# The down weights of a fused attention and feed-forward kernel: their rotation taken as eight products of rounded halves instead of four full float32 products

## The reference

```python
x = x + _L0_xattn_ref(_layernorm(x), ctx_2048, mask, Wq, bq, Wk, bk, Wv, bv, Wo, bo, gamma, beta, residual_scale)
x = x + _L0_ffn_ref(_layernorm(x), SU_ug, SU_dp, Wscale_ug, Wscale_dp, W_up, W_gate, W_down)

# _L0_ffn_ref
x = fwht(x * SU_ug) / SCALE                     # 512 wide
x_up = x @ W_up.T * (Wscale_ug[:INTER] * SCALE)
x_gate = x @ W_gate.T * (Wscale_ug[INTER:] * SCALE)
x = silu(x_gate) * x_up
x = fwht(x * SU_dp) / SCALE                     # 2048 wide
x = x @ W_down.T * (Wscale_dp * SCALE)
```

## Time and profile before

| | us |
|---|---|
| median of 3 runs | 1454.08 |
| lowest and highest run | 1452.18, 1454.42 |
| the profiled execution | 1452.16 |
| its span, first to last instruction | 1450.3 |
| TensorE busy | 1407.1 (97% of the span) |
| VectorE busy | 1107.4 (76%) |
| ScalarE busy | 814.2 (56%) |

### The profile page before, as it was taken

The page is one execution under the profiler, slowest core; times in us unless marked ns, Lnnn a source line. Parts: engine busy times, 40 slices in busy tenths (PEclk is TensorE's granted clock), DMA queues, the critical chain, the costliest instruction groups (busy, mean ns, idle before and its releaser), DMA issues. The chain is left out here.

```text
span 1450.3 us, 25099 instructions
## 1 busy us (share of the span) xinstructions
PE 1407.1 (97%) x10344; PEld 954.1 (66%) x10344; DVE 1107.4 (76%) x1655; ACT 814.2 (56%) x1018; POOL 88.8 (6%) x128
## 2 busy tenths in 40 slices
PE   7999999999999999999999999998999999999997
PEld 6787333788333688333689333586788888888886
DVE  6953999885999895899885899887866565656654
ACT  5345999535999635899635899534533333333330
POOL 1000000101000100000100000110010010000100
PEclk9999999999999999999999999999999999999999
DMA  8453000536100425000424500362345554454435
GB/s 275 151 185 153 9 10 10 177 104 218 52 10 10 147 98 190 21 17 10 141 74 175 241 17 10 97 240 86 146 147 208 189 182 149 163 208 176 174 145 174
DMA packets 54785, 180.91 MB, mean 125 GB/s; under 512 B 11168, under 2 KB 25760, under 8 KB 42384
## 3 DMA queue, kind: packets, MB, share of 16 engines
q1 hardware_dynamic: 39696, 116.08, 22.2%
q0 software_dynamic: 14976, 63.23, 12.7%
HBM read 111.97 MB, written 67.31 MB: 124 GB/s over the span
## 5 line engine op out<-in xcount | busy, mean ns | idle before, releaser
L960 ACT ACTIVATE cx_probs<-cx_sc,proj_mbias 128x1024 f32<-128x1024 f32 (+1 forms) x416 | 442.7, 1113 | 48.2 <-PE cx_sc L1234 24.6
L1103 DVE TENSOR_SCALAR cx_probs<-cx_probs 128x1024 f32<-128x1024 f32 (+1 forms) x416 | 269.8, 685 | 50.8 <-ACT cx_probs L960 49.0
L1069 DVE TENSOR_TENSOR cx_padd<-cx_probs,cx_probs 128x1024 f32<-128x1024 f32 x192 | 234.0, 1219 | 0.9
L1234 PEld LDWEIGHTS cx_sc<-cx_q,cx_kt 32*128 32x128 f32 (+1 forms) x2496 | 103.7, 180 | 192.2 <-ACT cx_probs L960 172.5
L1257 PE MATMUL cx_acc<-cx_probs,cx_vt 128*32 128x512 f32 (+1 forms) x1664 | 218.1, 596 | 3.8 <-DVE cx_probs L1103 3.8
L1234 PE MATMUL cx_sc<-cx_q,cx_kt 32*128 32x512 f32 (+1 forms) x2496 | 206.5, 425 | 10.2 <-ACT cx_probs L960 7.1
L140 PE MATMUL ff_yp<-hand_wds,ff_held 128*128 128x512 f32 x624 | 143.7, 389 | 0.1
L1702 DVE TENSOR_TENSOR ff_x<-ff_yp,ff_x 128x512 f32<-128x512 f32 x128 | 85.4, 688 | 68.5 <-PE ff_yp L140 57.6
L140 PEld LDWEIGHTS ff_yp<-hand_wds,ff_held 128*128 128x128 f32 x624 | 117.0, 188 | 24.8 <-DVE ff_kept L1765 0.5
L1269 PE MATMUL cx_tot<-cx_padd,cx_ones 128*32 128x256 f32 x1536 | 120.8, 390 | 0.0
L902 ACT ACTIVATE cx_kt<-cx_sc,proj_bk 128x256 fp32r<-128x256 f32 (+1 forms) x96 | 44.5, 478 | 74.6 <-PE cx_sc L140 74.2
(11 more groups left out here) (294 smaller groups left out, 2057.7 us busy)
## 6 DMA issues: line engine op xcount, KB each, us to landing
ff_x<-scr_x SPq DMA_DIRECT2D x32, 1024.0 KB, 5.0
scr_x<-ff_x SPq DMA_DIRECT2D x28, 1024.0 KB, 4.7
proj_raw<-in_ctxT SPq DMA_DIRECT2D x20, 512.0 KB, 5.7
hand_wds<-scr_wd POOLq DMA_DIRECT2D x7, 1024.0 KB, 9.9
scr_q<-cx_q SPq DMA_DIRECT2D x3, 2048.0 KB, 6.5
cx_wo<-scr_wo POOLq DMA_DIRECT2D x3, 2048.0 KB, 13.7
scr_xs<-cx_xs POOLq DMA_DIRECT2D x3, 2048.0 KB, 7.9
cx_q<-scr_q SPq DMA_DIRECT2D x3, 1536.0 KB, 10.8
```

The lines of the kernel that those rows point to most:

```text
L960: nc.scalar.activation(prob(N)[0:r], bank_of(n)[0:r], ACT.Exp, bias=mbias[0:r, b, t:t + 1], scale=SCALE).then_inc(exp_done, 1)
L1069: nc.vector.tensor_tensor(padd[z][(g * QP + j) % 2][:], prob(2 * i + z)[:], prob(2 * i + 2 + z)[:], ALU.add).then_inc(added[z], 1)
L1103: nc.vector.tensor_scalar(prob(N)[0:r], prob(N)[0:r], LOW, HIGH, ALU.max, ALU.min).then_inc(clip_done, 1)
L1234: last = nc.tensor.matmul(bank_of(2 * i + h // 2)[0:r, h % 2], kt[own, z, c, t * P:t * P + r], q[own, y, c], start=n == 0, stop=n == 2)
```

## The change

The Hadamard matrix and the share are both rounded to short halves. The matrix holds only ones and minus ones, so its short form is exact and has no low part: each of the four products of a share with it becomes two short ones, of the high and the low half of the share. The high halves are four instructions on ScalarE (`halve_hi`), the low ones four on VectorE (`halve_lo`); they lie in the share's own two tiles. Both stand after the keys of piece 2, and for the share ahead after the keys of piece 4. The short matrix `had_r`, until now made in piece 5, is made after the root of piece 2.

```diff
+    def short_hadamard(self, nc, act, r, b):
+        act.wait_ge(self.o_done, b * ST + ST)
+        for k in range(2):
+            nc.scalar.activation(r.had_r[:, k], self.had[:, 0], ACT.Copy, scale=1.0 - 2 * k).then_inc(self.had_r_done, 1)
+
     def butterfly_hi(self, nc, act, r, b):
-        for k in range(2):
-            nc.scalar.activation(r.had_r[:, k], self.had[:, 0], ACT.Copy, scale=1.0 - 2 * k).then_inc(self.fly_hi, 1)
...
+        self.halves = tile("half_hi", 1, F32R), tile("half_lo", 0, F32R)
...
-    def rotation(self, nc, pe, part):
+    def halve_hi(self, nc, act, part):
         if part == self.AHEAD:
-            pe.wait_ge(self.loaded, (part + 1) * 16)
+            act.wait_ge(self.loaded, (part + 1) * 16)
         else:
-            pe.wait_ge(self.fly, (part + 1 - (part > self.AHEAD)) * self.OPS)
+            act.wait_ge(self.fly, (part + 1 - (part > self.AHEAD)) * self.OPS)
+        for i in range(len(self.banks)):
+            own = slice(i * self.PER_BANK, (i + 1) * self.PER_BANK)
+            nc.scalar.activation(self.halves[0][:, own], self.fl[:, own], ACT.Copy).then_inc(self.half_hi, 1)
+
+    def halve_lo(self, nc, dve, part):
+        for i in range(len(self.banks)):
+            own = slice(i * self.PER_BANK, (i + 1) * self.PER_BANK)
+            dve.wait_ge(self.half_hi, part * len(self.banks) + i + 1)
+            nc.vector.tensor_tensor(self.halves[1][:, own], self.fl[:, own], self.halves[0][:, own].bitcast(F32), ALU.subtract).then_inc(self.half_lo, 1)
+
+    def rotation(self, nc, pe, part, had_r):
         for i, bank in enumerate(self.banks):
-            nc.tensor.matmul(bank, self.had[:, 0], self.fl[:, i * self.PER_BANK:(i + 1) * self.PER_BANK], start=True, stop=True).then_inc(self.turned, 1)
+            own = slice(i * self.PER_BANK, (i + 1) * self.PER_BANK)
+            pe.wait_ge(self.half_lo, part * len(self.banks) + i + 1)
+            nc.tensor.matmul(bank, had_r, self.halves[0][:, own], start=True, stop=False)
+            nc.tensor.matmul(bank, had_r, self.halves[1][:, own], start=False, stop=True).then_inc(self.turned, 1)
...
# ScalarE, later_piece
                     if p == 2:
                         chain.root(nc, act, b - 1, 0)
+                        chain.short_hadamard(nc, act, room, b - 1)
+                        down.halve_hi(nc, act, TURN[b])
+                    if b == 1 and p == 4:
+                        down.halve_hi(nc, act, down.AHEAD)
...
# VectorE, later_piece, after keys_lo
+                    if p == 2:
+                        down.halve_lo(nc, dve, TURN[b])
+                    if b == 1 and p == 4:
+                        down.halve_lo(nc, dve, down.AHEAD)
                     if p == 2:
                         chain.scaled(nc, dve, room, b - 1)
...
# TensorE, turn
                     if p == 2:
                         pe.wait_ge(chain.d_done, b * ST)
-                        down.rotation(nc, pe, TURN[b])
+                        pe.wait_ge(chain.had_r_done, b * 2)
+                        down.rotation(nc, pe, TURN[b], room.had_r[:, 0])
```

More of the change, by code:

```diff
@@ L196, in __init__ @@
         self.had = m.sb("had", [P, 2, P])
-        self.fly_hi, self.fly_lo = m.sem("fly_hi"), m.sem("fly_lo")
+        self.fly_hi, self.fly_lo, self.had_r_done = m.sem("fly_hi"), m.sem("fly_lo"), m.sem("had_r_done")
         self.bv, self.su, self.rs = m.sb("bv", [P, HC]), m.sb("su", [P, HC]), m.sb("rs", [P, 1])
@@ L377, in butterfly_lo @@
         for c in range(HC):
-            dve.wait_ge(self.fly_hi, b * (HC + 2) + c + 3)
+            dve.wait_ge(self.fly_hi, b * HC + c + 1)
             nc.vector.tensor_tensor(r.fs[:, 1, c], r.xR[:, c], r.fs[:, 0, c].bitcast(F32), ALU.subtract).then_inc(self.fly_lo, 1)
@@ L438, with __init__ @@
     OPS = 2 * (IC.bit_length() - 1) + 1
-    def __init__(self, m, slab, ahead, banks, had):
+    def __init__(self, m, slab, ahead, banks):
         def tile(name, at, dt=F32):
@@ L448, in __init__ @@
         self.hi, self.lo = tile("wdhi", 0, F32R), tile("wdlo", 1, F32R)
+        self.halves = tile("half_hi", 1, F32R), tile("half_lo", 0, F32R)
+        self.half_hi, self.half_lo = m.sem("down_half_hi"), m.sem("down_half_lo")
         self.ws = m.sb("ws_dp", [P, H])
-        self.banks, self.had = banks, had
+        self.banks = banks
         self.consts_in, self.ws_done, self.loaded, self.fly, self.turned, self.hi_done, self.lo_done, self.stored = (
@@ L723, in context @@
         VT = H * 4
-        down = DownWeights(m, qslab, (vslab + (TT - 8) * VT, vslab + (TT - 4) * VT), banks, chain.had)
+        down = DownWeights(m, qslab, (vslab + (TT - 8) * VT, vslab + (TT - 4) * VT), banks)
         qu = Queries(m, q, qslab, banks, chain, proj, bq, q_mo)
@@ L1296, in turn @@
                         pe.wait_ge(chain.d_done, b * ST)
-                        down.rotation(nc, pe, TURN[b])
+                        pe.wait_ge(chain.had_r_done, b * 2)
+                        down.rotation(nc, pe, TURN[b], room.had_r[:, 0])
                     if b == 1 and p == 4:
                         pe.wait_ge(chain.xT_done, b * HC)
-                        down.rotation(nc, pe, down.AHEAD)
+                        down.rotation(nc, pe, down.AHEAD, room.had_r[:, 0])
                 def out_free(b):
```

## The result

| | us | ratio to before |
|---|---|---|
| before, median of 4 runs | 1453.98 | |
| changed, median of 4 runs (1469.1 to 1470.41) | 1469.92 | 1.011, 95% interval 1.0096 to 1.0123 |
| changed, span of the profiled execution (before: 1450.3) | 1467.9 | |

The change makes the kernel 16 us slower, in every run. The forecast was 1463.3 us and at most 1468. The direction and the place were right, the size was not.

What follows compares the result with a forecast made beforehand. TensorE was taken to bound the contexts. Waits beyond the gain of 2.65 + 2.65 + 2.2 = 7.5 us, plus 1.7 for one clock fall, made +9.2 on 1454.08: 1463.3 us, range 1456 to 1468.

Steps and rivals of the forecast that it cites:

- The gain: Rotation of a share on TensorE: eight short products take 1.83 us instead of 3.43, 1.60 us less, 6.4 for four.
- VectorE's delay: After the keys of piece 2: VectorE's scaling starts 4.54 us late, 2.12 idle for ScalarE and 2.42 of work.
- What is late next: Behind piece 3's low keys: transposes and other later steps just fit, so contexts 2 and 3 cost 2.65 us each.
- rival 4: A later wait has less slack, so VectorE's whole 4.54 us is carried on in each context: 1467.7 us, chance 0.09.
- The share ahead: Context 1, its rotation after piece 4: TensorE waits 1.1 us for ScalarE's signs and is 2.2 us late in all.
- The clock: Three new TensorE waits of 4.3 us: one lets the clock fall, +1.7 us, bounds +0 and +5.1.
- Rival 2: Every one of the three TensorE waits lets the clock fall, 1.7 us each on 7.5: 1466.7 us, chance 0.18.
- the forecast without a fall: Contexts 1 to 3: 7.5 us of waits beyond the gain, with TensorE's clock kept: 1461.6 us.

Runs made afterwards that it cites:

- products_alone: Changed kernel without the low halves: eight short products, all of the high half, taken in ScalarE's idle time after piece 1 (result not right): 1448.38 us, ratio 0.9958.
- filled_store_later: Changed kernel with 30 overwritten TensorE products in piece 3 and GpSimd's store of the high part held until VectorE's first residual sum: 1459.06 us.
- filled: Changed kernel with 36 overwritten products added on TensorE in piece 3 of contexts 1 to 3: 1461.52 us, and once more 1462.18 us.
- halves_alone: Changed kernel that still takes both halves but rotates the full share with the old full-matrix products: 1467.15 us, ratio 1.0089.

## Why the prediction was wrong

**The gain: right.** 1.60 us a share forecast, 1.61 measured in the trace, 6.2 us in all by products_alone.

**VectorE's delay: right in kind, 0.6 us short.** Forecast 4.54 us: 2.12 idle and 2.42 of work, measured 1.95 and 2.42, and 5.1 us in all at the low keys of piece 3 (323.27 - 317.61, less the 0.5 ahead of context 1). What failed was the sentence "above, nothing in the rows makes it longer than 4.54". The changed order put a small instruction under GpSimd's issue, 0.66 us more: L110 came 5.0 us later and the issue 0.9 us earlier. I had followed the store of the low part, which waits for VectorE, and not that of the high part, which the faster rotation sets free sooner. TensorE went on 323.79 - 320.05 - 0.53 = 3.2 us late for the 2.65 forecast, and 3.2 again in each of contexts 2 and 3: 1.7 us over the forecast in all. (The bracket, 4.67 us for 4.3, counts from the modelled end of the row before.) filled_store_later gives the difference back.

**What is late next: right.** No new wait at the transposes or the first scores; rival 4 (1467.7 us, the whole delay carried) came near the number by luck.

**The share ahead: wrong by 1.1 us, on the good side.** I had TensorE wait for the signs. ScalarE ended them at 343.0 us, near the 342.3 forecast, but TensorE came 6.7 us late by then, at 345.2, and waited for nothing. In filled, where it came earlier, it did wait for them, 0.30 us.

**The clock: this is the step that failed.** I took "one fall in three waits, bounds none and all, +0 and +5.1 us", at 1.7 us each. All three waits lost it, one of them for nearly 7 us (3.0 us lost, over the price of a single fall), 6.1 us together (5.8 against filled), and the first scores lost it in all three contexts, 2.1 us more. The term was forecast at 1.7 and came to 8.2. Rival 2, at 1466.7 us, was the right story with too low a price: it took 1.7 us for every fall, and nothing for the first scores. The working behind the term was thin, too. It counted one fall at two like places, where the first scores of context 3, which kept the clock, make it one at three; and it held that idle time of a few us sometimes costs the clock without looking at a wait of that kind in context 0 of the kernel before (TensorE's row, then its window behind the wait, with the granted clock after the busy time):
```profile
57.91 5.29 PE L140 MATMUL cx_sc<-proj_wv,proj_cs_even 128*128 128x512 f32 x22 [2.67 <-DVE cx_kt L1054]
```

```profile
58.00:61.50 3.50, 3.50 (x16) 1.00 1.07 429
```

This wait of 2.67 us kept the clock, and so did the 2.83 us at the same place of the changed kernel. It would have spoken for few falls, so the price of 4.67 us could only be had by a run.

Against filled, which keeps the clock at the values, the forecast without a fall (1461.6 us) stands within 1 us, in part by luck: VectorE's delay was taken too short and the wait of the share ahead too long.

The whole, from the profiles: three waits less gain 9.6 us (3 x 3.2), the share ahead -1.6, clock at the values 6.1, first scores 2.1, and 1.4 that belongs to the executions (0.5 before context 1, 0.9 in the feed-forward): 17.6 us. Against the 9.2 forecast, the clock is 6.5 too much, the waits with the share ahead are 0.5 too much, and the 1.4 are the rest.

**Open.** Why the first scores lose the clock in three contexts of the changed kernel, in two of halves_alone and in one or none of the others. After a wait that had lost it, five contexts of six lost it again there; in the other eight profiles, six of 24 did. That the first fall brings the second on is suggested by this and not shown. Open too is what makes a wait costly, for its length alone doesn't decide: 0.35 and 1.96 us did not cost the clock in the profiled executions, 2.38 and 4.67 us did each time, three contexts each, but 2.67 and 2.83 us in context 0 did not.

## What to carry to other kernels

Work that shortens TensorE by asking the engines beside it for a rounding step pays only if that step fits into their idle time; look for that gap first (here 11.7 us on ScalarE, and on VectorE 1.4 us with 1.0 more in two gaps behind it, one piece earlier) and put the step there. The same 32 instructions on these two engines cost 16 us in one place and gained 5.5 to 8 in the other. Price a new wait of TensorE of 2 us or more with a lost clock on top: here 1.5 to 3 us after each wait that lost it, and 2.1 us more in the first scores of the changed kernel.

## What the runs showed of the hardware

- Idle time of 2.38 and 4.67 us on TensorE ahead of the values of piece 3 went with 3.4 to 6.8 us at 1.2 GHz in six of six contexts (halves_alone and changed kernel), while 2.67 and 2.83 us in context 0 (kernel before and changed) kept 2.4 GHz; filling the 4.67 us with useless products made the kernel 8 us faster.
- The issue of a DMA on GpSimd (1.13 us) stretched a VectorE TENSOR_SCALAR of 4 columns (L110) from 0.17 to 0.83 us, in each of three contexts, and in none once it was moved; a TENSOR_TENSOR of 4 columns (L108) inside the same issue kept its 0.16 us.
